# Order of gathers and waits of adds on GpSimd in the routed experts of an attention and mixture-of-experts kernel

## The reference

```
x = x + xattn(layernorm(x), ctx)        # 2048 rows of 256: causal attention, cross attention
                                        # over 1601 rows, a dense FFN, three layernorms
h = layernorm(x)                        # 2048 rows of 256
logits = h @ wg.T                       # 8 experts
topk_w, topk_idx = top_k(softmax(logits), 2);  topk_w /= sum(topk_w)
y_e = (silu(h @ w1[e].T) * (h @ w3[e].T)) @ w2[e].T      # hidden width 512
x = x + sum over the two chosen experts of  weight_e * y_e
```

## Time and profile before

| | us |
|---|---|
| median of 3 runs | 526.07 |
| lowest, highest | 524.92, 526.53 |
| profiled execution, whole time | 526.67 |
| its span, first to last instruction | 524.2 |
| PE busy | 496.8 (95%) |
| POOL busy | 278.0 (53%) |

### The profile page before, as it was taken

The page is one execution under the profiler, slowest core; times in us unless marked ns, Lnnn a source line. Parts: engine busy times, 40 slices in busy tenths (PEclk is TensorE's granted clock), DMA queues, the critical chain, the costliest instruction groups (busy, mean ns, idle before and its releaser), DMA issues.

```text
span 524.2 us, 10993 instructions
## 1 busy us (share of the span) xinstructions
PE 496.8 (95%) x3686; PEld 326.6 (62%) x3686; DVE 378.8 (72%) x978; ACT 286.7 (55%) x575; POOL 278.0 (53%) x312
## 2 busy tenths in 40 slices
PE   7899999999999999999999999999999899999970
PEld 3576766656666676766667776656666566666650
DVE  5899887588967668877889899997878444444440
ACT  4556767647466745773749657664454344433320
POOL 4463203003642708994496763545754756757573
PEclk9999999999999999999999999999999999999995
DMA  8002533246877537985598770248597689778683
GB/s 273 19 25 77 171 102 108 94 96 105 149 175 121 148 74 168 156 147 167 98 191 178 158 264 20 90 111 114 110 194 110 113 131 122 137 117 139 102 93 38
DMA packets 135313, 65.60 MB, mean 125 GB/s; under 512 B 109757, under 2 KB 126590, under 8 KB 135262
## 3 DMA queue, kind: packets, MB, share of 16 engines
q1 hardware_dynamic: 127774, 54.69, 48.6%
q0 software_dynamic: 7488, 10.23, 12.2%
HBM read 28.19 MB, written 10.35 MB: 74 GB/s over the span
## 4 chain that ended last, share of the span: by engine, by line
PE 58%; DVE 11%; DMA 8%; issue 8%; ACT 6%; POOL 4%; POOLq 2%; SPq 1%; DVEq 0%; ACTq 0%
PE ps L1205 47%; DMA out<-y,qst 5%; DMA probT<-prob 3%; PE ps L1300 3%; PE ps L1302 3%; PE ps L1301 3%; ACT ps L1016 2%; DVE cmax L1744 2%; POOL out L968 2%; POOLq L962 1%; POOL y L942 1%; ACT tT L1002 1%; ACT prob L1015 1%; PE ps L1214 1%; PE ps L1261 1%
## 5 line engine op out<-in xcount | busy, mean ns | idle before, releaser
L1205 PE MATMUL ps<-arena,probT 128*128 128x256 f16 (+2 forms) x1092 | 180.0, 318 | 4.0 <-issue 1.8
L1205 PEld LDWEIGHTS ps<-arena,probT 128*128 128x128 f16 (+1 forms) x1092 | 104.4, 97 | 61.0 <-issue 8.3
L1205 PE MATMUL ps<-arena,qT 128*128 128x512 f16 (+1 forms) x384 | 69.1, 332 | 1.0 <-DVE prob L1885 0.7
L968 POOL DMA_INDIRECT out<-y,qst x39 | 62.9, 1612 | 13.1 <-issue 7.8
L1015 ACT ACTIVATE prob<-ps,nbias 128x512 f16<-128x512 f32 x64 | 39.0, 609 | 50.9 <-DVE nbias L1750 50.9
L1143 ACT ACTIVATE w1m<-ps 128x512 f32<-128x512 f32 x39 | 23.3, 598 | 74.7 <-PE ps L1205 56.6
L1205 PE MATMUL ps<-arena,tT 128*128 x468 | 57.4, 273 | 0.9 <-DVE tT L2445 0.6
L791 POOL TENSOR_TENSOR rstd<-veps,expo 128x1 f32<-128x1 f32 x16 | 9.0, 563 | 91.8 <-DVE veps L1779 91.8
L1205 PEld LDWEIGHTS ps<-arena,qT 128*128 128x128 f16 x384 | 32.5, 97 | 36.0 <-issue 1.7
L942 POOL DMA_INDIRECT y<-hrow,qst x39 | 40.4, 1037 | 24.1 <-DVE qst L2107 12.8
L1205 PE MATMUL ps<-tT 128*128 128x512 f16 (+3 forms) x234 | 48.8, 346 | 1.4 <-DVE probT L1810 0.8
(11 more groups left out here) (240 smaller groups left out, 919.5 us busy)
## 6 DMA issues: line engine op xcount, KB each, us to landing
stage<-we_in SPq DMA_DIRECT2D x33, 256.0 KB, 3.0
prob<-we_in SPq DMA_DIRECT2D x15, 256.0 KB, 3.8
xin<-x_in SPq DMA_DIRECT2D x16, 128.0 KB, 2.7
out<-y SPq DMA_DIRECT2D x16, 128.0 KB
hrow<-tT SPq DMA_DIRECT2D x4, 512.0 KB, 3.5
y<-x_in SPq DMA_DIRECT2D x3, 512.0 KB, 7.6
stage<-z_in SPq DMA_DIRECT2D x4, 256.0 KB, 5.7
prob<-w_in SPq DMA_DIRECT2D x4, 256.0 KB, 3.2
```

The costliest lines, as they stand in the source:

```text
L968: g.indirect_dma_start(out[:rows_of(p), :], bass.IndirectOffsetOnAxis(ridx[:, n:n + 1], 0), ys[:, n % RING, :], None, compute_op=ALU.add). ...
L1205: r = t.matmul(o, lhs(a), rhs(b), start=first and n == 0, stop=last and n == 2)
```

## The change

Five edits, all in the routed part:

1. `GATHERS_FROM[2]` goes from 10 to 12: list 3's gathers (and with them the lead of two more, LEAD) begin at round 12.
2. Gathers 5, 6 and 7 are issued ahead of the last of the small powers (`rstd_of("n_", NB - 1)`); before, 5 came behind it and 6 and 7 in round 1. They still wait for PE's transposes of tiles 1, 2 and 3.
3. In `add(n)` the register is loaded first, ahead of all waits.
4. A second table `before2` is made by one more DVE operation in each list. Where n mod 4 is 1 (except n = 5) `add(n)` loads a second register from it and waits for n - 2 up to that number, in place of the constant wait.
5. The small operation on `gap` (128x1, a multiplication whose result nobody reads) now stands behind all waits of an add, that for `e_y` included, right ahead of the transfer, and in every add; before, it stood ahead of the wait for `e_y`, and only in adds with a register.

```diff
-GATHERS_FROM = {1: 4, 2: 10}
+GATHERS_FROM = {1: 4, 2: 12}
...
             def add(n):
                 p = phase_of(n)
+                alone = n <= RING or n == PHASES[p][1]
+                if not alone:
+                    if n == PHASES[p][1] + 1 or n == RING + 1:
+                        wait(pool, "r_next", p + 1)
+                    done = pool.value_load(before[0:1, n:n + 1], min_val=16, max_val=16 * NJ)
+                    if n % RING == 1 and n > RING + 1:
+                        done2 = pool.value_load(before2[0:1, n:n + 1], min_val=16, max_val=16 * NJ)
                 wait(pool, "x1_out", 16 * TB * PHASES[p][0])
-                alone = n <= RING or n == PHASES[p][1]
                 if n > 2:
                     add_done(n - 3)
-                if n > 1 and (alone or n % RING == 1):
+                if n > 1 and (alone or n == RING + 1):
                     add_done(n - 2)
                 if n and alone:
                     add_done(n - 1)
                 if not alone:
-                    if n == PHASES[p][1] + 1 or n == RING + 1:
-                        wait(pool, "r_next", p + 1)
-                    done = pool.value_load(before[0:1, n:n + 1], min_val=16, max_val=16 * NJ)
                     pool.wait_ge(sm[f"e_add{(n - 1) % RING}"], done)
                     if n % RING != 1:
                         pool.wait_ge(sm[f"e_add{(n - 2) % RING}"], done)
-                    g.tensor_tensor(gap[:, n:n + 1], expo[:, 0:1], expo[:, 0:1], ALU.mult)
+                    elif n > RING + 1:
+                        pool.wait_ge(sm[f"e_add{(n - 2) % RING}"], done2)
                 wait(pool, "e_y", n + 1)
+                g.tensor_tensor(gap[:, n:n + 1], expo[:, 0:1], expo[:, 0:1], ALU.mult)
                 g.indirect_dma_start(out[:rows_of(p), :], ...
...
             gather(3)
             gather(4)
+            gather(5)
+            gather(6)
+            gather(7)
             rstd_of("n_", NB - 1)
-            gather(5)
             gates(2)
             weigh(2)
-            issued = 6
+            issued = 8
...
+                m0 = max(n0, 1)
+                v.scalar_tensor_tensor(before2[:, m0 + 1:n1], differ[:, m0 + 1:n1], 16.0, adds[:, m0 - 1:n1 - 2],
+                                       ALU.mult, ALU.add)
```

More of the change, by code:

```diff
@@ L265, in xattn_ffn_moe @@
         before = inside(qst, 7 * NJ, [P, NJ], U32)
+        before2 = inside(u, 400, [P, NJ], U32)
         tkey = inside(qst, 8 * NJ, [P, NJ])
```

## The result

| us | before | after |
|---|---|---|
| median (15 runs each) | 526.07 | 529.92 |
| lowest, highest | 524.92, 530.15 | 528.59, 532.95 |
| profiled execution, whole time | 526.67 | 529.55 |
| its span | 524.2 | 527.8 |
| start of the last add | 515.96 | 519.55 |

The ratio is 1.0082, with a 95% interval of 1.0063 to 1.0100: **slower by 0.8%**, 3.85 us. The forecast was 527.7, and the range, which ended at 529.4, missed the median by 0.5 us. From the start of the last add to the end of the run it is 10.0 us now, as against 10.7.

The account below looks back on a forecast made before the run. PE sets the pace up to 485 us, POOL's chain of adds the end. PE's last-add time 510.3 plus slip 6.65 (3.85 waiting, 2.8 clock) gives 516.95; plus 10.7, 527.7 us. Range 524.2 to 529.4.

Parts of the forecast that it names:

- The gather of 17: On POOL, behind tile 10's add, it would start at 411.85 instead of 405.53, its rows landing at 414.95.
- PE's idle: Ahead of tile 17's transposes PE would stand from 409.7 to 414.95, 5.2 us, waiting for the gather.
- slip: PE's delay from tile 17 on: 3.85 us plus 2.8 for the clock, 6.65; below 5.7 the end needn't move.
- Rival 1: After PE's stop the clock falls briefly or not at all; the delay of 3.85 stays hidden, 525.0 us; chance 0.25.
- 2: Tile 17's gather lands 2 us later; PE stops for 7 us and is 8.6 late, 529.6 us; chance 0.08.
- 3: PE isn't held at all; POOL's chain of adds carries its 3 us lead to the end, 522.1 us; chance 0.07.
- Tile 37: Its add, with the second table, would start 1.94 us behind tile 36's instead of 3.48, a gain of 1.54.
- the early gathers: Gathers 5 to 7 ahead of the last power use POOL's free 8 us; gains are lost at tile 3: 0.
- DVE's new operations: Three more small operations of 0.18 us each on DVE, behind the lists' signals: 0, at most 0.5 us.
- what would show it: Profile signs: PE idle about 5 us before tile 17, clock 0.50, w1 product 5 us, last add released by DVE's product.
- the price of the clock: After PE's stop, work at half rate would lose 2.2 to 3.4 us; 2.8 taken, from matmuls at the program's start.
- the sentence on the register loads: In POOL's chained adds the load already precedes the wait that counts, transfer 0.34 us after the small operation: no gain.

## Why the prediction was wrong, step by step

**Right.** The gather of 17 (412.68; said 411.85) and its consequences: PE's idle 6.10 (5.2), the clock falls, slip 6.87 (6.65), PE's end 515.67 (515.8). At tile 18 the slip is 6.2: 4.3 of waiting, where 3.85 had been said, and 1.9 of the clock. Rival 1, that the clock holds, is out, and so are 2 (a late landing: it took 2.9 from the gather's start to the transposes) and 3. Tile 37 gained its 1.54, and the early gathers cost nothing; DVE's new operations were not run alone. Of the rows that "what would show it" asked for, those on PE's stop, its clock and the adds of 9 and 10 came true (406.26 and 410.82, where 405.0 and 409.9 had been said). Two didn't: the w1 product of 5 us (3.12), and the one on the end of the run, "the last add released by the product of tile 38 on DVE". In this trace that product was begun at 516.03, 3.5 us ahead of the add.

**Right in part by luck: the price of the clock.** The 2.8 was the middle of a reading at the start of the program, an array at half rate for 4.45 to 6.9 us of work. Behind the stop PE worked at the lower clock for 3.7 us only (415.56 to 419.3), half of which is 1.9, and 1.93 is what the kernel with PE kept busy shows at tile 18. The rest of its 2.8 came later, on a way that the sum didn't have. The reading itself was weak: the profile gives the granted clock at the start as 1.00, so that only the lengths of the matmuls speak for the lower one there, and the six at 8.75, taken as the end of it, were themselves still slow (1.93 against 1.47).

**The step that failed** is the sentence on the register loads: "in the chained adds the load is already ahead of the wait that counts, so nothing is gained there". Nothing was gained; but that the landing's wait stood first behind the load was the asset, and that the edit gives the first place to `x1_out`, was not asked. The cost was set at 0 without a bound. It is 0.45 to 0.5 us in each chained add (landing to transfer 0.87 to 0.92 instead of 0.42), and 6.8 us by the run with these edits alone. The row "small operation released, transfer 0.34 later" was read as a constant of the machine; it was the result of the waits' order. That this is the step, and not the sum for PE, shows in the kernel with edit 1 alone: there the add of tile 36 starts at 512.52, released by its product, and two steps of 1.94 behind it, which edit 4 allows, would be 516.4; the prediction had 516.95.

**A second slip, of no effect on the number.** How PE's delay holds POOL was worked out with a slip of 3.85, before the clock's 2.8 had been added, and not done again; and it was read at tile 27. The place is tile 14, where the gather of 24 waits for the transposes of 20:

```profile
430.88 0.96 POOL L943 DMA_INDIRECT y<-hrow,qst  x1 [2.98 <-PE ps L1539]
```

PE's transposes of 20 came at 430.22 instead of 423.50, and the add of 14 at 432.46, 2.24 behind them; 2.4 had been said. At tile 27 the gather ahead of the add had no wait for PE (idle 0.31), so the chain was POOL's own there. With the slip of 6.65 the add of 14 would have been put at 423.50 + 6.65 + 2.4 = 432.55. From there it is 84.5 to the last add as before (431.45 to 515.96), less the 1.54: 515.5, still ahead of PE's 516.95, and the same forecast. The measured stretch is 87.1 (432.46 to 519.55), **4.1 longer than those 83.0**. Eight chained adds with a register lie in it (16, 19, 21, 23, 25, 28, 30 and 33), each with its 0.45 to 0.5: 3.6 to 4.0. That is the size of the failed step, but that the two agree so well is luck: single steps differ from those before by -1.7 (tile 21) to +1.5 (tile 33), since landings differ, and in the changed kernel with the landing first this stretch is 85.1 and not 83.0.

**Why the failed step cost less than its 6.8.** The parts don't add: +1.3%, +0.25%, perhaps +0.4% and nothing make +0.8%. With the lists at 10 the place of one wait moves the last add by 10.8 (524.80 and 513.99), with the lists at 12 by 4.6 (519.55 and 514.98). By the timelines, edit 1 takes the wait for the list out of POOL's chain, which is 2.3 us ahead at tile 10; while the chain is late this is gain, and its longer steps ahead of tile 14 are then hidden by the wait for PE. Forecast as the one large loss, edit 1 is a small loss where the steps are short (1.0025) and a gain where they are long (1.0144 without it, 1.0082 with it).

**On the clock.** The Trainium skill (TensorE: Matmul & The Clock Gate, section "HAM oscillation — how this bites in real kernels") says that a PE that waits for data between bursts is throttled and starts the next burst cold; the traces agree, in the middle of the kernel too, with 6.1, 4.7 and 3.2 us of idle each followed by a granted clock of 0.50, and none after 0.9.

## What to carry to other kernels

Moving a wait, even one that is met long before, can change which wait an instruction carries and which ones hold the sequencer. On POOL put the wait that really waits first behind the last instruction; that the next transfer is then set up during it is the reading that fits all runs here. When a change touches the order of waits, look at the sequencer's semaphore rows before and after, not only at the engine's, and ask which waits have a row, not how long the rows are. And give every edit costed at nothing a bound by the row that it would move, here 0.34 times 17 adds, 5.8 us.

## What the runs showed of the hardware

- POOL, landing to the next dependent transfer by way of a small operation: 0.42 us when the landing's wait stands first, 0.82 to 0.92 when another does. The other waits are semaphore instructions of the sequencer. They take 17 or 43 ns when met and up to 4.0 us when they hold, but one that starts only once it is met shows 17 ns as well (L967 in the kernel with edits 3 and 4 alone).
- One wait more in each of 32 adds, always met, made the kernel 1.6% slower.
- PE's clock: after stops of 6.1, 4.7 and 3.2 us the granted clock was at the lower level for 6.8, 6.8 and 3.4 us; with 50 matmuls on ones in place of the stop of 6.1 us the clock held, PE was 1.93 us earlier at the next tile and 2.8 us earlier at its end.
- Adds that follow each other with neither a wait nor a gather between them start 1.94 us apart. The landing of an add took from 3.6 to about 7 us after its start; with a transposing transfer issued in its first microsecond the median was 4.9, with none near it 3.8.
